# Windowed attention and an LSTM-like cell: the softmax division in the values product's layout, and ScalarE as the sender of the query and key parts

## The reference, cut to what matters

```
qkv = einsum('bse,fe->bsf', x, w_in);  q, k, v = split(qkv, 3)
p = softmax(q @ k.T / 4 + bias, window of 128 + 128 keys)
o = (p @ v)                       # [b, 16 heads, 512, 16]
x = layernorm(x + o.reshape(b, s, e) @ w_out.T)
# the rows of x are then steps t of a gated cell with state c:
c = sigmoid(x[t] @ wf.T + c @ uf.T + bf) * c + sigmoid(x[t] @ wi.T + c @ ui.T + bi) * tanh(x[t] @ wc.T + c @ uc.T + bc)
x = layernorm(x + tanh(x @ wo.T + c_final @ uo.T + bo))
```

## Time and profile before

| | before |
|---|---|
| median of 3 runs (lowest, highest) | 994.1 us (992.67, 994.81) |
| the profiled execution: own time, span | 994.83 us, 992.7 us |
| TensorE busy, matmuls | 911.2 us, 92% of the span |
| VectorE, ScalarE, GpSimd busy | 714.1, 574.8, 409.0 us |
| DMA, share of 16 engines | 45.3% on SyncE's queue |

### The profile page before, as it was taken

How to read it: one execution, slowest core, us unless ns; L and a number is a source line. 1 busy time by engine, 2 the same in 40 slices (tenths; PEclk the granted TensorE clock), 3 DMA queues, 4 the chain that set the end, 5 groups by cost and what they waited for, 6 DMA issues and landing times. The chain is left out here.

```text
span 992.7 us, 25986 instructions
## 1 busy us (share of the span) xinstructions
PE 911.2 (92%) x9500; PEld 749.7 (76%) x9500; DVE 714.1 (72%) x2795; ACT 574.8 (58%) x1167; POOL 409.0 (41%) x687
## 2 busy tenths in 40 slices
PE   3587889999999999999999999999999999989994
PEld 2365668888888888888888888888787876668884
DVE  7666677878787868787878787878787754337875
ACT  6044556565656565656565656565656554335786
POOL 6143343444535353535353535354444443001443
PEclk8586989999999999999999999999999989899998
DMA  7644454535454545353645454645444400131764
GB/s 265 164 124 127 131 139 132 151 122 156 124 151 128 145 134 150 123 154 125 153 128 151 128 143 137 149 131 147 133 121 138 119 23 22 44 106 46 215 204 131
DMA packets 93534, 131.86 MB, mean 133 GB/s; under 512 B 12128, under 2 KB 47584, under 8 KB 93408
## 3 DMA queue, kind: packets, MB, share of 16 engines
q1 hardware_dynamic: 93136, 129.95, 45.3%
q10 hardware_dynamic: 272, 0.26, 0.1%
HBM read 79.31 MB, written 50.33 MB: 131 GB/s over the span
## 5 line engine op out<-in xcount | busy, mean ns | idle before, releaser
L689 DVE CUSTOM_DVE_ANT_0 bank<-bank,mask 128x256 f32<-128x256 f32 (+1 forms) x1024 | 369.4, 423 | 130.7 <-PE bank L951 128.7
L448 ACT ACTIVATE Pt<-bank 128x512 f32<-128x512 f32 (+1 forms) x512 | 248.2, 536 | 193.4 <-PE bank L972 193.3
L347 POOL TENSOR_SCALAR_AFFINE_SELECT Pt<-Pt 128x512 f32<-128x512 f32 x256 | 170.4, 666 | 403.9 <-ACT Pt L448 403.9
L951 PE MATMUL bank<-Ks,Qs 59*128 59x256 f32 (+1 forms) x1024 | 148.2, 319 | 44.9 <-DVE max_q L689 31.3
L951 PEld LDWEIGHTS bank<-Ks,Qs 59*128 59x128 f32 x1024 | 107.3, 191 | 86.6 <-DVE max_q L689 42.5
L689 DVE DVE_READ_ACCUMULATOR2_ANT max_q<- 128x1 f32 x1024 | 144.9, 142 | 0.0
L349 POOL TENSOR_SCALAR_AFFINE_SELECT Pt<-Pt 128x384 f32<-128x384 f32 x256 | 144.7, 565 | 0.0
L986 PE MATMUL bank<-Pt,Vp 128*32 128x256 f32 (+1 forms) x2048 | 130.9, 377 | 0.0
L932 PE MATMUL bank<-x1T,Wg 64*128 64x512 f32 x960 | 127.9, 398 | 1.0 <-DVE o_tok L703 1.0
L932 PE MATMUL bank<-cT,Ug 64*128 64x512 f32 x960 | 125.7, 393 | 0.0
L972 PE MATMUL bank<-Qs,Ks 60*128 60x256 f32 (+1 forms) x1024 | 111.8, 271 | 0.7 <-ACT Pt L448 0.3
(11 more groups left out here) (111 smaller groups left out, 1354.7 us busy)
## 6 DMA issues: line engine op xcount, KB each, us to landing
parts_dram<-qk_parts SPq DMA_DIRECT2D x128, 256.0 KB
Qs<-parts_dram SPq DMA_DIRECT2D x128, 128.0 KB, 2.7
Ks<-parts_dram SPq DMA_DIRECT2D x128, 128.0 KB, 2.8
xt_raw<-in_xt SPq DMA_DIRECT2D x16, 512.0 KB, 4.5
Qs<-parts_dram SPq DMA_DIRECT2D x128, 64.0 KB, 2.7
Ks<-parts_dram SPq DMA_DIRECT2D x128, 64.0 KB, 2.7
x_res<-in_x SPq DMA_DIRECT2D x16, 512.0 KB, 3.9
x_dram<-y SPq DMA_DIRECT2D x16, 512.0 KB, 4.4
```

Source lines behind the costliest of these rows:

```text
L347: gp.affine_select(out=p4[:, :, 0:128], in_=p4[:, :, 0:128], compare_op=ALU.is_ge, fill=0.0, base=0, pattern=[[0, 4], [1, 128]], channel_m ...
L448: sc.activation(probabilities(g, 2 * pair + odd)[:, S * a:S * a + n], SC[odd][:, 0:n], ACT.Exp).then_inc(exp_done, 1)
L689: ins = ve.tensor_tensor_reduce(out=raw, in0=raw, in1=mask[:, keys], scale=1.0, scalar=MASKED, op0=ALU.add, op1=ALU.max, accum_out=max_q[: ...
L951: ins = te.matmul(MX[odd][:, 256 * (n % 2):256 * (n % 2) + 256][:, keys], Qs[rows, 2 * g + pair, n * WIN:(n + 1) * WIN], Ks[rows, 2 * g + ...
```

## The change

The division moves to where the values product leaves its result, with channels as rows. ScalarE stores each group's copy to DRAM right after `ctx_out`. SyncE loads the channel rows into `o_un` (`load_contexts`) and the 16 denominator rows, cut in four, into `den_q` (`load_denominators`). VectorE turns `den_q` so that 128 partitions share the work, inverts it and turns it back; SyncE stores the inverses and reads them again, each row 16 times (`spread_inverses`); GpSimd multiplies (`scale_contexts`). For sequences 0 to 14 the 24 transposes and the eight VectorE instructions of `normalise` are gone; sequence 15 keeps the old way.

The eight issues of `parts_to_dram` for a next sequence move from SyncE to ScalarE: four after `max_row(t, 1)`, ahead of `attend(8)`, and four after `attend(14)`. Those of sequence 0 stay. On SyncE `max_to_stack(t, 0)` goes ahead of `stack(t, 2)`. The parts of x for t + 2 are made in iteration t, the low ones by GpSimd. `pairs_of` swaps one bank instead of two pairs, and gates 0 and 1 take B1 and A1. The weights Wo and Uo of the closing loop take the place of Win and are made at the end (`last_weights_hi`, then GpSimd).

```diff
+            moving = PAIRS[1]
+            return (moving[t % 2], PAIRS[0][1]), (PAIRS[0][0], moving[1 - t % 2])
 
...
+            def load_denominators(t):
+
+                sp.wait_ge(den_cleared, 1)
+                for g in range(QUADS):
+                    wait(sp, ctx_stored[g], 16, t, 16)
+                wait(sp, inv_stored, 16, t - 1, 16)
+                rows = ctx_dram[t % 2].rearrange("g (h r) (q i) -> q (g h) r i", r=2 * D, i=128)[:, :, D, :]
+                for q in range(4):
+                    sp.dma_start(den_q[32 * q:32 * q + H, :], rows[q]).then_inc(den_in, 16)
+
+            def load_contexts(t, c):
+                for g in (2 * c, 2 * c + 1):
+                    wait(sp, ctx_stored[g], 16, t, 16)
+                wait(sp, otlo_done, 2, t - 1, c + 1)
+                rows = ctx_dram[t % 2, 2 * c:2 * c + 2].rearrange("g (h r) s -> (g h) r s", r=2 * D)[:, 0:D, :]
+                sp.dma_start(o_un[:, c, :], rows).then_inc(o_un_in[c], 16)
+
+            def store_inverses(t):
+                wait(sp, inv_turned, 1, t, 1)
+                sp.dma_start(inv_dram[t % 2].rearrange("r (q i) -> q r i", i=128), den_q[:, :]).then_inc(inv_stored, 16)
+
+            def spread_inverses(t):
+
+                wait(sp, inv_stored, 16, t, 16)
+                for c in range(KC):
+                    wait(sp, scaled_done, 2, t - 1, c + 1)
+                    rows = inv_dram[t % 2, 8 * c:8 * c + 8]
+                    sp.dma_start(inv_den[:, c, :], rows.unsqueeze(1).to_broadcast([8, D, S])).then_inc(inv_in[c], 16)
+
...
                 if p1: max_to_stack(t - 1, 3)
                 if now: stack(t, 1)
                 if p2:
                     wait(sp, y_done, 2, t - 3, 2)
                     sp.dma_start(x_res[:, :, :], x[t - 2].rearrange(tok, p=128)).then_inc(xres_in, 16)
+                if by_rows: load_contexts(t - 1, 0)
                 if real(t + 2): load_xt(t + 2)
                 if now:
+                    max_to_stack(t, 0)
                     stack(t, 2)
-                    max_to_stack(t, 0)
                     stack(t, 3)
-                if n1: parts_to_dram(t + 1, 0)
                 if now: max_to_stack(t, 1)
                 if p2:
                     wait(sp, x1_done, 4, t - 2, 4)
                     sp.dma_start(x1_dram[t - 2].rearrange(tok, p=128), y[:, :, :]).then_inc(x1_out, 16)
+                if by_rows: load_denominators(t - 1)
                 if n1: stack(t + 1, 0)
+                if by_rows: load_contexts(t - 1, 1)
                 if now: max_to_stack(t, 2)
-                if n1: parts_to_dram(t + 1, 1)
+                if by_rows:
+                    store_inverses(t - 1)
+                    spread_inverses(t - 1)
+                if t == B - 1: load_last_weights()
 
...
+            def scale_contexts(t, c):
+
+                wait(pool, o_un_in[c], 16, t, 16)
+                wait(pool, inv_in[c], 16, t, 16)
+                gp.tensor_tensor(o_un[:, c, :], o_un[:, c, :], inv_den[:, c, :], ALU.mult).then_inc(scaled_done, 1)
...
                     for hh in range(4):
                         window(t, 1, hh)
 
             for t in range(B + 2):
...
+            def parts_to_dram(t, c):
+
+                for g in (2 * c, 2 * c + 1):
+                    wait(act, stacked[g], 16 * STACK_DMAS, t - 2, 16 * STACK_DMAS)
+                for which in range(2):
+                    wait(act, qklo_done, 4, t, 2 * c + which + 1)
+                    for part in range(2):
+                        sc.dma_start(parts_dram[t % 2, c, which, :, part, :, :],
+                                     qk_parts[:, c, which, part, :].bitcast(F32)).then_inc(parts_out[c][which], 16)
 
...
             def ctx_out(t, g, bank):
                 wait(act, pv_ready, 4, t, g + 1)
-                wait(act, ct_ready, 4, t, g)
+                pt, pg = before(t, g)
+                if pt < B - 1:
+                    wait(act, ctx_stored[pg], 16, pt, 16)
+                else:
+                    act.wait_ge(ct_ready, g)
                 sc.activation(ctx_raw[:, :], bank[:, :], ACT.Copy).then_inc(ctx_done, 1)
-
-            def ot_hi(t, c, bank):
+                if t < B - 1:
+                    wait(act, ctx_done, 4, t, g + 1)
+                    sc.dma_start(ctx_dram[t % 2, g], ctx_raw[:, :]).then_inc(ctx_stored[g], 16)
+
+            def ot_hi(t, c):
...
                     wait(act, op_ready, 2, t - 1, 2)
-                wait(act, ot_ready, 2, t, c + 1)
+                wait(act, scaled_done, 2, t, c + 1)
+                sc.activation(oT[:, 0, c, :], o_un[:, c, :], ACT.Copy).then_inc(othi_done, 1)
...
+            def last_weights_hi():
+
+                act.wait_ge(last_weights_in, 32)
+                act.wait_ge(v_ready, 2 * B)
+                sc.activation(out_stage[:, 1, :], out_stage[:, 1, :], ACT.Copy, scale=0.5).then_inc(u_o_halved, 1)
+                sc.activation(Wo[:, 0, :, :], out_stage[:, 0, :].rearrange("p (c n) -> p c n", c=KC), ACT.Copy).then_inc(last_hi, 1)
+                act.wait_ge(u_o_halved, 1)
+                sc.activation(Uo[:, 0, :, :], out_stage[:, 1, :].rearrange("p (c n) -> p c n", c=KC), ACT.Copy).then_inc(last_hi, 1)
...
                     gates(t - 3, 5, A1)
                 max_row(t, 1, B0)
+                if n1: parts_to_dram(t + 1, 0)
                 attend(8)
...
+                    x1_hi(t - 2, 1, B0)
                 attend(14)
+                if n1: parts_to_dram(t + 1, 1)
                 attend(15)
 
...
+            def turn_denominators(t):
+
+                wait(dve, den_in, 64, t, 64)
+                ve.transpose(den_t[:, :], den_q[:, :]).then_inc(den_turned, 1)
+
+            def invert_denominators(t):
+                wait(dve, den_turned, 1, t, 1)
+                own = den_t[:, :].rearrange("p (b r) -> p b r", r=32)[:, :, 0:H]
+                ve.reciprocal(own, own).then_inc(den_inverted, 1)
+
+            def turn_inverses(t):
+                wait(dve, den_inverted, 1, t, 1)
+                ve.transpose(den_q[:, :], den_t[:, :]).then_inc(inv_turned, 1)
+
...
                 attend(13)
+                if p1: turn_denominators(t - 1)
                 if n1: qk_lo(t + 1, 3, B1)
-                if p1: normalise(t - 1, 3, A0)
-                if p2:
-                    x1_lo(t - 2, 0, B0)
...
                 if p1:
-                    freed(pe, (x1lo_done, 2, t - 3, 1), (qklo_done, 4, t, 3))
-                    max_transpose(t - 1, 3, A0)
-                    freed(pe, (x1lo_done, 2, t - 3, 2), (qklo_done, 4, t, 4))
-                    values(t - 1, 1, A1)
-                    wait(pe, maxrow_done, 4, t - 1, 4)
-                    ctx_transpose(t - 1, 0, A0)
-                if p2:
-                    wait(pe, gate_done, 6, t - 3, 1)
-                    o_transpose(t - 2, 0, B0)
-                    freed(pe, (gate_done, 6, t - 3, 2), (ctx_done, 4, t - 1, 1))
-                    o_transpose(t - 2, 1, B1)
+                    freed(pe, (x1lo_done, 2, t - 3, 2), (qklo_done, 4, t, 3))
+                    max_transpose(t - 1, 3, B0)
+                    freed(pe, (x1lo_done, 2, t - 3, 1), (maxrow_done, 4, t - 1, 3))
+                    values(t - 1, 1, B1)
 
...
-                    wait(pe, o_done, 4, t - 1, 1)
...
+                    wait(pe, gate_done, 6, t - 3, 2)
                     abreast(g2, g3, 0, None)
```

256 lines of the change are left out of this document (143 added, 113 removed).

## The result

The changed kernel takes 1089.5 us (median of four runs, 1082.8 to 1092.6); the kernel before, beside it, 994.5 (992.7 to 997.6). The ratio is 1.094, with a 95% interval from 1.089 to 1.100: 9.4% slower, where 977 was forecast, in a range up to 1003.

The account below looks back on a forecast made before the run. TensorE, busy 92% of the span, was taken to bound the kernel. 13 full iterations at -1.24 us (-16.1), with the other iterations, start (-1.5) and end (+0.8), gave -17.9 from 994.83: 977 us, range 950 to 1003.

Parts of the forecast that it names:

- I count nothing: Way from last context through DRAM to ot_hi: 3 us to spare at best, 0.7 missing at worst, priced at zero.
- rival 2: Inverses come late at ot_hi(t - 2, 0), holding exps of attend(2) and scores of attend(3): 1009 us, chance 13%.
- the issues on ScalarE: Ahead of attend(8): four take 3.38 us, starting between 395.8 and 396.6; TensorE waits 2 us, the place loses 1.25.
- Rival 1: ScalarE's issues don't hold its work up: 961 us at minimum issue times, 949 with nothing held up; chance 22%.
- the 0.2 us for four: Estimate for four issues from the skill's 50 ns per dispatch; would make the sum some 28 us lower; set aside.
- the walk: Step-by-step times behind the issues, from attend(8) to attend(11), which starts at 403.8 against 402.53 before.
- The second wait of 0.5: TensorE's smaller wait for exps, forecast behind the one of about 2 us in scores of attend(9).
- The second four: Issues behind attend(14), 410.9 to 414.3: cost nothing, covered by the gates' products with 0.5 us to spare.
- the sum: A full iteration changes by -1.88 - 0.41 + 1.25 - 0.2 = -1.24 us, times 13 is -16.1.
- What comes off TensorE: Transposes and a wait: 1.88 us after attend(0), 0.41 after attend(5), 0.59 after attend(8), 0.49 for a fourth group.
- The end: last_weights_hi puts three copies ahead of the last layer norm: 1.8 us lost, 1.0 won, together 0.8 lost.
- rival 3: ScalarE's issues hold up more: 989 us if they start only at 396.6, 1019 at the longest issue times; chance 17%.

Follow-up runs that it names:

- e4: The changed kernel without loading, turning, inverting, storing or spreading denominators; GpSimd multiplies by ones, contexts still go through DRAM: 1004.2 us.
- e7: The changed kernel with GpSimd multiplying by ones and not waiting for the inverses; all transfers and SyncE's waits stay: 1085.4 us.
- e13: e7 without SyncE's waits ahead of the denominators' loads and the spreading loads, which read rows of x instead: 1040.6 us, ratio 1.045.
- e15: e13 with the stores of parts issued by SyncE again: 1000.5 us, ratio 1.002 to the kernel before.
- e5: e4 with the stores of parts issued by SyncE again: 974.2 us, against 998.2 for the kernel before beside it.
- e3: The kernel before with only the stores of parts moved to ScalarE, at the change's places: 1020.8 us against 999.5.
- e9: The changed kernel with parts on SyncE, denominators turned earlier, SyncE's list reordered, second row of maxima ahead of the first four stores of parts: 1046.5 us.
- e1: The changed kernel with the third row of maxima moved ahead of stack(t + 1, 0) and load_contexts(t - 1, 1) on SyncE: 1113.4 us.

## Why the prediction was wrong

**Wrong, and the main fault: "I count nothing"** for the new way from the last context to `ot_hi`. It costs 85 us (e4). Three things in that step failed.
- It followed the chain's data and asked when `ot_hi` gets it, and the rival made of it (rival 2) had its place there. e7 shows 4 us for that. What it did not ask is what is queued behind the waits: "SyncE loses eight issues and gains eight smaller ones" counts issues and no waits. (It counts them wrong too: nine are gained, and four of them are of 256 KB, as large as those lost.) SyncE stands 200 us for the two landings, and `stack(t + 1, 0)` and the third and fourth row of maxima are behind them; that is 45 us (e7 against e13).
- It took landings of 2.7 to 4.4 us, from an execution in which one queue issued nearly everything in order. The context's store took 7.2 behind a megabyte of parts from the same list, the inverses' store 7.5 beside the next megabyte. The prediction itself put each of them right behind four such stores, in its walks of `attend(8)` and `attend(14)`, and did not carry that into the landing. For the data it mattered little up to the inverses, which were ready 21.5 us behind the layer norm and not 20.0; for SyncE's list, which stood all that time, it mattered much.
- It gave the chain's transfers and issues no price for what they do to others: 36 us (e13 against e4), 26 with the parts on SyncE (e15 against e5), with two of the waits left out. They are 9.4 of the 32.9 MB more, and how much of the 36 is their bytes stays open.

The Trainium skill has a rule for the second point, in the section that the prediction weighed for another purpose, "Issuing engines are not separate DMA queues" of "DMA: Bandwidth & Descriptors": transfers run on the same 16 engines and interleave, whichever engine started them. The trace agrees: the row of maxima issued on SyncE at 459.52, beside ScalarE's stores, let TensorE go only at 467.63. The rows of maxima together, in SyncE's old list, made TensorE wait 0.3 us in the whole run before.

**Right in its mechanism, a little small: the issues on ScalarE.** 3.4 us were forecast for the four and 3.4 came, starting 0.2 behind the early end of the bounds; the wait in `scores` of `attend(9)` was 2 and is 2.15 to 2.27. Rival 1 (they hold nothing up) is refuted by e3, and the 0.2 us for four, worked out from a figure that the Trainium skill states for GpSimd's path, by the 3.4. In e4's iteration at 404.89, where the clock stays at 1.00, the raw scores of `attend(11)` start 416.07 - 404.89 = 11.18 behind the layer norm, 402.53 - 393.34 = 9.19 before: the place loses 1.99, where 1.25 were said. Of the 0.74 more, 0.28 is that `scores` of `attend(9)` start that much later than in the walk, and the rest lies in `attend(10)`: there the walk took the old 1.67 from `scores` to `attend(11)`, but it is now 416.07 - 413.93 = 2.14. The products behind these `scores` start at 414.58, 0.65 later than they, where it was 401.04 - 400.86 = 0.18 before. The first `scores` start just behind the first half of the `exps` (413.30 and half of 1.06), the next products just behind the second half; so the term left out is most likely this second half, which the walk followed on ScalarE and not into TensorE. The second wait of 0.5 that was forecast doesn't appear as a row for this reason. The second four do cost nothing through ScalarE's own list: no wait for `exps` stands in `attend(15)` of a full iteration, in e4 or in the changed kernel.

**Missing: the clock.** Behind a wait of 2 us TensorE often runs at the lower level for a while. In e4's iteration at 504.89 the 24 products behind the wait take 2.40 and the 22 of the next group 2.05, against 1.58 and 1.64 for 24 and 23 before. It isn't so in each iteration, and what decides it no run here shows: in the twelve of e4 from 203.31 to 803.16 eight have a mean clock of 0.97 and four 1.00, and the eight last some 0.85 longer. That is 0.5 an iteration. The layer norms of e4 start at 203.31 and 854.45, 50.09 an iteration where the sum says 50.05 - 1.24 = 48.81. These 1.3 are the 0.74 above and the 0.5 of the clock; times 13 they are 17 of the 27 us between the forecast and e4. Another 7 lie ahead of the first layer norm (150.24; by the terms for the start, iterations 0 and 1 it should start at 142.60 - 1.5 + 1.85 + 0.15 = 143.1). e5 with the parts on SyncE has 144.35 there; the mean granted clock of the first 140 us is 0.72 in e4, 0.77 in e5 and 0.78 before, so the issues with their clock are the likely cause. In the changed kernel the clock costs far more, since it also follows the waits for the maxima: the 29 us of busy time in the 85.

**What comes off TensorE: right beside ScalarE's issues, covered without them.** In e4 the sum closes with the gain as it was forecast. Without the issues and the chain, by the prediction's own terms, 1.88 + 0.41 + 0.59 + 0.2 = 3.1 us an iteration go; in e5 only 50.05 - 48.61 = 1.44 went. 17.3 us in 13 waits for maxima are in e5, 1.3 an iteration, which the kernel before doesn't have, and two iterations behind waits of 2.53 and 2.18 have a clock of 0.97 and last 51.0 and 50.9. TensorE comes to the second row of maxima a little earlier, but the larger part is that the row is later: in the iteration at 435.49 SyncE gets to it as long behind the layer norm as before (3.38), and its two transfers then take 3.42 us to issue, 1.94 before. No part of the prediction names this wait.

**The end.** TensorE waits 5.6 where it waited 4.0 for the layer norm of the earlier trace rows: 1.6 more, 1.8 was said. From the last layer norm on nothing changed.

**The chances.** The side was wrong with 72% on it. Of the 22% for slower, some 9 points stood on rival 2, to which e7 leaves some 4 us in this kernel, and 9 on rival 3, which the 3.4 us for four issues refute; the loss came by a way that no rival named.

## What to carry to other kernels

When a change adds a wait for a landing to a list that also issues small urgent transfers, don't ask first who needs the data that lands, but what is queued behind the wait, and for how long it stands; here the second cost 45 us and the first some 4. A landing depends on what was issued just ahead of it, on its own queue and here on the other one too: a duration read in an execution with less ahead of it is a lower bound. And a wait of TensorE in the forecast has to be priced with the slower products that can follow it: here 0.85 us behind two of three waits of 2.2, and a third of the 85 us in all.

## What the runs showed of the hardware

- Issuing takes longer when much is under way: two transfers of 4 KB took 1.31 us of SyncE's list, and 2.96 to 3.38 beside or behind a megabyte of stores; four of 8 KB took 1.71, 5.46 behind such stores in e9, and 6.54 in e13.
- A wait of TensorE of 2.16 us was followed by a mean granted clock of 0.72 over six us (e4), with 1.00 ahead of it. Of 13 waits of 2.15 to 2.87 us in e4 nine were followed by a lower clock, and four of 12 waits of 1.56 to 1.78 in e3.
- In the changed kernel an issue on ScalarE began at 440.37 while ScalarE's arithmetic of 440.24 to 440.92 was still under way.
- Moving one tiny transfer ahead (e1) made the program 24 us slower, since the larger one that it displaced landed beside the stores.
